# The layer norm, gating sums and beta projection between a feed-forward and a linear attention moved into the attention's first units, and the next layer norm moved into its last steps

## The chip, the cores and the metric

The kernel runs on one core of one Trainium2 chip. The metric is the device time of one execution in microseconds (us). The kernel before took 1204.1 us in the median of three runs, from 1202.74 to 1205.73 us.

## The reference

The input is x, four batches of 512 tokens with 256 features. Four layers are added to it one after the other, and each but the third reads a layer norm of x:

```python
x = x + attn_a(layernorm(x))      # 16 heads of 16, softmax over a batch
x = x + ffn(layernorm(x))         # feed-forward "b"
x = x + attn_b(layernorm(x))      # linear attention, 16 heads of 128
x = x + ffn(layernorm(x))         # feed-forward "d"
```

The feed-forward routes each token to two of eight experts, but its result is added to only eight rows of x (rows 0 to 7 of batch 0, since the scatter is by expert number): `out.at[indices[:, k]].add(gates[:, k] * silu(silu(x w1) w3) w2)`. So the kernel sums the gated hidden rows by expert first, and multiplies by w2 only eight rows.

The linear attention projects q, k, a gate and v, passes q and k through a causal convolution with four taps, a silu and a layer norm over the head, and keeps a state `S = (1 - b) S + b v k` with `b = sigmoid(x Wb + bb)` for each head and token; the output is `S q`, times the silu of the gate, times Wo.

## The kernel before, in words

Tokens stand on 128 partitions: x_tok holds 16 tiles of 128 tokens, four tiles to a batch. The normed x is kept transposed, as xn_hi and xn_lo (two parts of an fp32 number, and a product of two such numbers takes three matmuls). Each stage is a block in which five engines run their own list of instructions in the order in which the code writes them, with semaphores between them. At a block's end all engines meet at a barrier. PE is the matmul engine, ACT the scalar engine, DVE the vector engine, POOL is GpSimd, and SP issues DMAs.

A layer norm (`layer_norm`, L61) goes in groups of one batch: `statistics` on DVE (four BN_STATS, L83, and four BN_AGGR, L86), `deviations` on POOL (a power of -0.5, L96 and L98), `normalise` on DVE (L106), `transpose` on PE (L130), `high_parts` on ACT (L116) and `low_parts` on DVE (L121).

The stages that matter here, in order:

- `norm_and_ffn` with tag b (L868). PE ends with the products of w3 (L992), then the gated sums (L1020, 32 matmuls), their transpose (L1026), and the product with w2 (L1030); DVE adds the eight rows to x_tok (L1124).
- All semaphores are cleared, with a barrier (L1812).
- `norm_and_decay` (L1127). Tile 0 of x_tok is normed again, since its rows changed. For the batches 1, 2, 3, 0, PE projects beta (L1184), ACT takes the sigmoid (L1198), PE turns it to token order (L1172), DVE forms 1 - b and its running products (L1211, L1217), and SP writes them to keep_rows in DRAM (L1157).
- `linear_attention` (L1260). 64 units: 8 pairs of heads, and in a pair 8 units (batch and head of the pair). The work of a unit is spread over 7 steps, so that step u does the projections of unit u (L1477, L1490), transposes u-1 (L1504) and u-2 (L1511), scores u-2, reads out u-3 (L1555, L1558), multiplies by Wo for u-5 (L1579) and adds u-6 to x_tok (L1707). "Step" and "unit" are counted from 0, so the steps 64 to 69 are the drain, in which no projection is left.
- `norm_and_ffn` with tag d. It starts with the statistics of batches 0 and 1 on DVE; PE's first products are the router's (L960) for batch 0, then come the transposes of batch 1 and the products of w1 (L980). The transposes of batches 2 and 3 lie between later products.

In the linear attention one chain goes from unit to unit: ACT normalises q and k of unit u-1 (L1612), PE turns them back (L1511), ACT applies the affine part (L1628) and scales the projection by the first tap (L1595), DVE adds the other taps (L1679), PE transposes, DVE takes the statistics (L1718), and POOL forms the scales (L1399 to L1413), for which ACT waits to normalise the next. Two waits of DVE's gating step matter for the drain (`gated` is a single buffer):

```python
if has(u, 3):
    v, r = u - 3, (k - 3) % 4
    wait(dve, read_out, v + 1)
    wait(dve, gate_act, v + 1)
    wait(dve, gated_lo_done, v)
    dve.tensor_tensor(gated[:], outp[:], gate[:, r, :], ALU.mult).then_inc(gated_done, 1)
```

`gated_high` on ACT (L1635) and `gated_low` on POOL (L1451) split that buffer for the product with Wo.

## Time and profile before

| | us |
|---|---|
| median of three runs | 1204.1 |
| the profiled execution, its own time | 1201.73 |
| span in its profile | 1199.9 |
| feed-forward b, from its first matmul | 295.67 |
| first instruction of `norm_and_decay` | 341.93 |
| first matmul of the linear attention | 355.66 |
| last addition of the linear attention begins | 1146.48 |
| first statistics of feed-forward d | 1147.49 |
| first router matmul of feed-forward d | 1156.24 |

The last six rows are points on the profile's time axis, counted from the span's start. The span is the time from the first to the last recorded instruction; the profiled execution took 1.83 us more than its span. PE is busy for 1131.8 of 1199.9 us, but a share like that is a mean over stages: it is nearly full in the middle of the linear attention and has gaps where one stage hands over to the next.

### The profile page before, as it was taken

To read this page: it belongs to the slowest core of one execution; us is meant where nothing else is said; L and a number is where in the kernel's file an instruction comes from. 1 tells how busy PE (TensorE), PEld (TensorE's weight loads), DVE (VectorE), ACT (ScalarE), POOL (GpSimd) and SP (SyncE) were. 2 spreads that over 40 slices of the span, in tenths; PEclk is the share of its full clock that TensorE was granted. 3 is DMA by queue.
4 is the path that set the end of the run, shared out by engine and by line. 5 is a ranking of instruction groups with operands and counts; after the bars stand their busy time and mean duration, and the time that the engine had idled before them with its cause. 6 is when DMAs were issued, how large, how long until landed. Compare 5 with 4: busy or idle time off the path is not lost. (4 is left out here: it accounts for less than half of the span.)

```text
span 1199.9 us, 22451 instructions
## 1 busy us (share of the span) xinstructions
PE 1131.8 (94%) x7558; PEld 909.3 (76%) x7558; DVE 923.5 (77%) x2124; ACT 772.1 (64%) x1533; POOL 634.6 (53%) x1078
## 2 busy tenths in 40 slices
PE   8999999888977999999999999999999999999768
PEld 7444434337646899999999999999999999999646
DVE  6888877846437788888888888888888888888452
ACT  3377767772436776777676777676777777776323
POOL 4020500001703777786777786777787687767520
PEclk9899999998989999999999999999999999999989
DMA  6434434401111012101110201111211211111020
GB/s 181 54 54 55 54 54 55 54 2 37 77 34 56 31 47 68 47 32 51 63 47 32 82 32 47 67 48 32 81 35 45 76 38 43 35 47 33 16 70 1
DMA packets 23449, 60.50 MB, mean 50 GB/s; under 512 B 3367, under 2 KB 8359, under 8 KB 22183
## 3 DMA queue, kind: packets, MB, share of 16 engines
q1 hardware_dynamic: 23335, 59.07, 18.9%
q8 instruction: 61, 1.00, 0.4%
q14 instruction: 53, 0.43, 0.1%
HBM read 44.67 MB, written 2.33 MB: 39 GB/s over the span
## 5 line engine op out<-in xcount | busy, mean ns | idle before, releaser
L1679 DVE SCALAR_TENSOR_TENSOR ln_xn<-l_proj_q,par,ln_xn 128x511 f32<-128x511 f32 (+2 forms) x192 | 142.6, 742 | 113.1 <-ACT ln_xn L1595 110.8
L688 DVE TENSOR_REDUCE a_neg_max<-a_scores 128x1 f32<-128x512 f32 x244 | 155.1, 683 | 38.6 <-PE a_scores L416 36.8
L607 ACT ACTIVATE a_probs<-a_scores_t 128x512 f32<-128x512 f32 x256 | 138.4, 600 | 61.0 <-PE a_scores_t L435 60.0
L1601 ACT ACTIVATE ln_xn<-ln_xn,par 128x512 f32<-128x512 f32 x128 | 92.5, 723 | 91.2 <-DVE ln_xn L1679 91.2
L1421 POOL TENSOR_TENSOR l_k_tok<-l_normed,k_norm 128x384 f32<-128x384 f32 x64 | 64.9, 1014 | 157.9 <-ACT l_normed L1612 157.9
L1679 DVE SCALAR_TENSOR_TENSOR ln_xn<-l_proj_k,par,ln_xn 128x511 f32<-128x511 f32 (+2 forms) x192 | 143.0, 745 | 4.5
L1612 ACT ACTIVATE l_normed<-l_turn_q,l_shift,l_scale 128x128 f32<-128x128 f32 x256 | 96.3, 457 | 26.1 <-POOL l_shift L1413 26.0
L1411 POOL TENSOR_TENSOR l_scale<-l_small,l_minus_half 128x8 f32<-128x8 f32 x64 | 105.0, 1641 | 5.0
L1612 ACT ACTIVATE l_normed<-l_turn_k,l_shift,l_scale 128x128 f32<-128x128 f32 x256 | 97.1, 481 | 0.0
L1555 PE MATMUL l_outp<-l_masked,l_values 128*128 128x128 f32 x512 | 88.6, 275 | 0.9 <-DVE x_tok L1707 0.9
L1654 ACT ACTIVATE l_gate<-l_proj_gv 128x512 f32<-128x512 f32 x64 | 38.2, 597 | 79.0 <-PE l_proj_gv L1477 79.0
L1686 DVE TENSOR_TENSOR_SCAN l_decay<-l_keep,ident 128x128 f32<-128x128 f32 x256 | 87.2, 403 | 0.0
L1451 POOL TENSOR_TENSOR l_gated_lo<-l_gated,l_gated_hi 128x512 fp32r<-128x512 f32 x64 | 82.4, 1288 | 7.3 <-ACT l_gated_hi L1635 7.3
L435 PE MATMUL a_scores_t<-a_stack 50*128 50x512 f32 x256 | 73.4, 490 | 7.8 <-ACT a_probs L607 5.4
L1490 PE MATMUL l_proj_gv<-head_hi,xn_hi 128*128 128x256 f32 x256 | 76.6, 299 | 2.1 <-ACT l_gate L1654 2.1
L1579 PE MATMUL l_outp<-wo_hi,l_gated_hi 128*128 128x256 f32 x256 | 72.9, 285 | 4.1 <-DVE l_gated L1736 2.4
L89 POOL MEMSET ln_minus_half<- 128x4 f32 x3 | 0.3, 101 | 141.0 <-POOLq L170 135.2
L1558 PE MATMUL l_outp<-l_q_late,l_state 128*128 128x128 f32 x384 | 74.2, 275 | 0.0
L435 PEld LDWEIGHTS a_scores_t<-a_stack 50*128 50x128 f32 x256 | 28.5, 184 | 60.0 <-ACT a_probs L607 40.0
L1555 PEld LDWEIGHTS l_outp<-l_masked,l_values 128*128 128x128 f32 x512 | 72.7, 192 | 1.1 <-issue 1.1
L96 POOL TENSOR_SCALAR ln_var_eps<-ln_mean_var 128x4 f32<-128x4 f32 x12 | 3.0, 254 | 133.0 <-DVE ln_mean_var L79 94.2
L1497 PEld LDWEIGHTS l_scores<-l_qk 128*128 128x128 f32 x512 | 67.5, 193 | 6.5 <-issue 1.5
(321 smaller groups left out, 3606.9 us busy)
## 6 DMA issues: line engine op xcount, KB each, us to landing
l_keep<-keep_rows SPq DMA_DIRECT2D x64, 448.0 KB, 3.6
a_stack<-a_dense SPq DMA_DIRECT2D x90, 128.0 KB, 5.1
head_raw<-w_heads SPq DMA_DIRECT2D x8, 1024.0 KB, 6.7
x_tok<-x SPq DMA_DIRECT2D x4, 512.0 KB, 8.6
wo_raw<-w_o SPq DMA_DIRECT2D x1, 2048.0 KB, 11.4
out<-x_tok SPq DMA_DIRECT2D x1, 1920.0 KB
a_stack<-a_max_rows_t SPq DMA_DIRECT2D x64, 4.0 KB
ctx_tok<-w_qkv SPq DMA_DIRECT2D x1, 768.0 KB, 7.0
```

Of the source, the lines that this page charges most:

```text
L435: pe.matmul(scores_t[q % TURNS][:], half_rows(k_stack[i], e, STACK + 2)[:, slot, t * P:(t + 1) * P], half_rows(q_stack[i], e, STACK + 2)[: ...
L607: act.activation(probs[:, n % 2, h, :], scores_t[(4 * n + h) % TURNS][:], ACT.Exp, scale=SOFT_SCALE).then_inc(probs_done, 1)
L688: dve.tensor_reduce(neg_max[:, g % 2, at:at + 1], max_bank(g, j), AX.X, ALU.max, negate=True).then_inc(max_done, 1)
L1411: pool.tensor_tensor(scale[:, i, :], small[:, 7, :], minus_half[:], ALU.pow).then_inc(scales_ready, 1)
L1451: pool.tensor_tensor(gated_lo[:, k % 4, :], gated[:], f32(gated_hi[:, k % 4, :]), ALU.subtract).then_inc(gated_lo_done, 1)
L1490: last = pe.matmul(proj_gv[:, t * PAIR:(t + 1) * PAIR], lhs, rhs, start=(j == 0), stop=(j == 3 * KD - 1))
L1555: last = pe.matmul(outp[:, tok], values[:, c % 2, t, e * DK:(e + 1) * DK], masked[:, m, tok], start=True, stop=(t == 0))
L1558: last = pe.matmul(outp[:, tok], state[:, m, t - 1, :], q_late[:, m, (t - 1) * P:t * P], start=False, stop=True)
L1601: act.activation(conv[:, w, m, :], conv[:, w, m, :], ACT.Silu, bias=par[:, h, 2 * TAPS + w:2 * TAPS + w + 1]).then_inc(act_sem[w], 1)
L1612: last = act.activation(normed[:, w, t, :], turn[w][:, t * P:(t + 1) * P], ACT.Identity, scale=scale[:, m, j:j + 1], bias=shift[:, m, j:j ...
L1679: ins = dve.scalar_tensor_tensor(conv[:, w, m, s:], proj[w][:, 0:SEQ - s], par[:, h, tap:tap + 1], conv[:, w, m, s:], ALU.mult, ALU.add)
L1686: last = dve.tensor_tensor_scan(decay[:, tok], keep[:, r, tok], ident[:], 0.0, ALU.mult, ALU.add)
```

## The change

`norm_and_decay` is gone, and its work is written into the first steps of `linear_attention`. Feed-forward b ends after its gates: the gated sums, their transpose, the product with w2 and the addition to x_tok are written into step 0 of the linear attention. Hidden rows, slots and the fold matrix live on through the barrier (`carried`), and the two parts of beta's weights are made inside feed-forward b (one ACT and one DVE instruction). In the pairs 0 to 6 the batches come in the order 1, 2, 3, 0, so that batch 0, which waits for the sums, is needed last; in the last pair they come in the order 0, 1, 2, 3.

By step: step 0 has beta of batch 1 (projection, sigmoid, turn, running products), the gated sums, fold and expert rows, and the statistics of tile 0. Step 1 has the rest of tile 0's norm, the beta projections of batches 2, 3 and 0, and at ACT's end of the step their three sigmoids. Step 2 has the twelve turns of beta on PE, and DVE forms the running products of one batch in each of the steps 2, 3 and 4, each followed by SP's write to DRAM and, in SP's queue, by the load that reads it back.

At the other end, the layer norm of feed-forward d (`ln_d`) is set up before the linear attention, and batches 0, 1 and 2 are normed in the steps 64 to 69 and right behind them. Feed-forward d then starts at its router and norms only batch 3.

```diff
 def linear_attention(...)
+        def batch_of(u):
+            place = u % BODY // 2
+            return place if u >= UNITS - BODY else beta_order[place]
...
         @block.gpsimd
+                if u == 1:
+                    ln.deviations(pool, 0)
+                if u == UNITS + 1:
+                    ln_d.deviations(pool, 0)
...
             steps(step, 4)
+            for g in range(1, NB - 1):
+                ln_d.deviations(pool, g)
...
         @block.tensor
+            def project_beta(b):
+                tok, j = slice(b * SEQ, (b + 1) * SEQ), 0
+                for kd in range(KD):
+                    for lhs, rhs in split_passes(beta_hi[:, kd, :], beta_lo[:, kd, :], xn_hi[:, kd, tok], xn_lo[:, kd, tok]):
+                        last = pe.matmul(beta_bank[b][0:LH, :], lhs, rhs, start=(j == 0), stop=(j == 3 * KD - 1))
+                        j += 1
+                last.then_inc(beta_z, 1)
...
             def step(pair, k, u, of):
+                if u in (UNITS + 2, UNITS + 4):
+                    ln_d.transpose(pe, (u - UNITS - 2) // 2, proj)
+                if u == 0:
+                    project_beta(1)
...
+                    if u == 0 and w == 0:
+                        turn_beta(1, chunks)
+                if u == 0:
+                    sum_gated()
...
+                if u == 1:
+                    ln.transpose(pe, 0)
...
+                if u == 0:
+                    fold_sums()
+                if u == 1:
+                    wait(pe, rows_added, 1)
+                    project_beta(2)
+                    wait(pe, ln.lo_done, KD)
+                    project_beta(3)
+                if u == 2:
+                    for b in beta_order[1:]:
+                        turn_beta(b, outp)
...
+                if u == 0:
+                    expert_rows()
+                if u == 1:
+                    project_beta(0)
...
             steps(step, 6)
+            ln_d.transpose(pe, NB - 2, proj)
...
         @block.scalar
+                if u == 0:
+                    sigmoid(1)
+                if u == UNITS + 2:
+                    ln_d.high_parts(act, 0, proj)
...
+                if u == 1:
+                    for b in beta_order[1:]:
+                        sigmoid(b)
...
         @block.vector
+                if u == 1:
+                    ln.normalise(dve, 0)
+                if u == UNITS + 5:
+                    ln_d.normalise(dve, NB - 2)
+                if u in (2, 3, 4):
+                    keep_of(beta_order[u - 1])
...
+                if u in (UNITS + 2, UNITS + 4):
+                    ln_d.low_parts(dve, (u - UNITS - 2) // 2, proj)
+                if u in (UNITS + 1, UNITS + 3):
+                    ln_d.normalise(dve, (u - UNITS - 1) // 2)
+                if u in (UNITS, UNITS + 2, UNITS + 4):
+                    wait(dve, added, UNITS - BODY + 2 * ((u - UNITS) // 2 + 1))
+                    ln_d.statistics(dve, (u - UNITS) // 2)
```

ACT's list before, from the end of step 1 into step 2 of the linear attention (L1612 normalises unit 0, L1628 and L1595 are the affine part and the first tap that follow):

```order
L1654 ACTIVATE l_gate<-l_proj_gv 128x512
L1601 ACTIVATE ln_xn<-ln_xn,par 128x512 x2
L1612 ACTIVATE l_normed<-l_turn_q,l_shift,l_scale 128x128 x4
L1612 ACTIVATE l_normed<-l_turn_k,l_shift,l_scale 128x128 x4
L1628 ACTIVATE l_qk<-l_turn_q,norm 128x512
L1595 ACTIVATE ln_xn<-l_proj_q,par 128x512
L1628 ACTIVATE l_qk<-l_turn_k,norm 128x512
L1595 ACTIVATE ln_xn<-l_proj_k,par 128x512
```

ACT's list now, at the same place (the line numbers have shifted, L1630, L1646 and L1613 are the same three; L1657 is the sigmoid):

```order
L1684 ACTIVATE l_gate<-l_proj_gv 128x512
L1619 ACTIVATE ln_xn<-ln_xn,par 128x512 x2
L1630 ACTIVATE l_normed<-l_turn_q,l_shift,l_scale 128x128 x4
L1630 ACTIVATE l_normed<-l_turn_k,l_shift,l_scale 128x128 x4
L1657 ACT_TABLE_LOAD
L1657 ACTIVATE hidden<-l_outp,beta_bias 16x512
L1657 ACTIVATE hidden<-l_chunks,beta_bias 16x512
L1657 ACTIVATE hidden<-l_scores,beta_bias 16x512
L1646 ACTIVATE l_qk<-l_turn_q,norm 128x512
L1613 ACTIVATE ln_xn<-l_proj_q,par 128x512
L1646 ACTIVATE l_qk<-l_turn_k,norm 128x512
L1613 ACTIVATE ln_xn<-l_proj_k,par 128x512
```

Two high parts of tile 0 have come in ahead of the gate, and a table load and three sigmoids stand between the normalising and the affine part; a second table load brings the silu back.

DVE's list before, from step 65 of the drain into feed-forward d (L1736 gates, L1697 carries the state, L1707 adds to x_tok, L1278 and L1064 are the block's end and the next one's beginning):

```order
L1736 TENSOR_TENSOR l_gated<-l_outp,l_gate 128x512
L1697 SCALAR_TENSOR_TENSOR l_state<-l_state,l_keep,l_chunks 128x128 x2
L1707 TENSOR_TENSOR x_tok<-l_outp,x_tok 128x512
L1736 TENSOR_TENSOR l_gated<-l_outp,l_gate 128x512
L1707 TENSOR_TENSOR x_tok<-l_outp,x_tok 128x512 x3
L1278 UNCONDITIONAL_BRANCH
L1064 UNCONDITIONAL_BRANCH
L83 BN_STATS ln_stats<-x_tok 128x6 x4
L86 BN_AGGR ln_mean_var<-ln_stats 128x2 x4
L83 BN_STATS ln_stats<-x_tok 128x6 x4
L86 BN_AGGR ln_mean_var<-ln_stats 128x2 x4
L106 TENSOR_SCALAR ln_xn<-x_tok,ln_mean_var,ln_rstd 128x256 x4
```

DVE's list now, from the end of step 65 (L106) into step 69 (L1768 adds to x_tok, L1812 gates):

```order
L106 TENSOR_SCALAR ln_xn<-x_tok,ln_mean_var,ln_rstd 128x256 x4
L1768 TENSOR_TENSOR x_tok<-l_outp,x_tok 128x512
L1812 TENSOR_TENSOR l_gated<-l_outp,l_gate 128x512
L121 TENSOR_TENSOR xn_lo<-l_proj_q,xn_hi 128x512
L121 TENSOR_TENSOR xn_lo<-l_proj_k,xn_hi 128x512
L83 BN_STATS ln_stats<-x_tok 128x6 x4
L86 BN_AGGR ln_mean_var<-ln_stats 128x2 x4
L1768 TENSOR_TENSOR x_tok<-l_outp,x_tok 128x512
L106 TENSOR_SCALAR ln_xn<-x_tok,ln_mean_var,ln_rstd 128x256 x4
L1768 TENSOR_TENSOR x_tok<-l_outp,x_tok 128x512
L121 TENSOR_TENSOR xn_lo<-l_proj_q,xn_hi 128x512
L121 TENSOR_TENSOR xn_lo<-l_proj_k,xn_hi 128x512
```

What stood behind the four last additions now stands between them: normalise, low parts and statistics of one batch after the other.

## Rows read from the trace of the kernel before

**Rows 1.** Busy time in stretches; columns: stretch, length, busy and count per engine, clock, DMA.

```profile
335.00:356.00 21.00, 13.51 (x85) 6.03 (x84) 9.27 (x29) 6.06 (x11) 1.19 (x6) 0.87 0.06 11
...
411.00:1111.00 700.00, 698.72 (x5056) 645.58 (x5055) 597.20 (x1414) 505.50 (x1029) 522.61 (x911) 1.00 0.15 49
...
355.60:360.50 4.90, 4.84 (x12) 3.82 (x13) 0.99 (x2) 0.69 (x1) 0.15 (x2) 0.50 0.79 188
...
1156.20:1158.80 2.60, 2.56 (x7) 0.87 (x8) 2.60 (x12) 0.00 (x0) 0.85 (x2) 0.50 0.02 6
```

**Rows 2.** Timeline from feed-forward to linear attention; columns: start, duration, engine, line, operation.

```profile
335.38 1.08 ACT L1062 ACTIVATE f_hidden_b<-f_mid_b 128x512 f32<-128x512 f32 x2
...
335.68 1.93 PE L1020 MATMUL f_sums_b<-f_hidden_b,f_slots_b 128*32 128x256 f32 x32 [0.32 <-DVE f_slots_b L1118]
...
339.10 1.03 PE L1030 MATMUL f_sums_b<-w,f_summed_t_b 128*8 128x256 f32 x4 [0.27 <-DVE f_summed_t_b L1122]
...
340.17 0.41 DVE L1124 TENSOR_TENSOR x_tok<-f_sums_b,x_tok 8x256 f32<-8x256 f32 x1 [1.12 <-PE f_sums_b L1030]
...
341.93 0.20 POOL L1162 MEMSET d_zeros<- 16x128 f32 x1 [14.79 <-POOLq L1812]
...
349.36 0.68 ACT L1198 ACTIVATE d_beta_rows<-d_z,beta_bias 16x512 f32<-16x512 f32 x1 [1.16 <-PE d_z L1184]
...
352.36 1.04 DVE L1217 TENSOR_TENSOR_SCAN d_keep<-d_keep,d_zeros 16x128 f32<-16x128 f32 x3
...
355.66 0.77 PE L1477 MATMUL l_proj_q<-xn_hi,head_hi 128*128 128x512 f32 x1 [3.32 <-PEq L1131]
```

**Rows 3.** Stretch with the six matmuls of one beta projection, line 1184 alone.

```profile
347.76:349.12 1.36, 1.36 (x6) 0.48 (x6) 1.00 0.25 42
```

**Rows 4.** Timeline of the first four units of the linear attention.

```profile
361.77 1.28 ACT L1654 ACT_TABLE_LOAD   x1
...
363.06 0.60 ACT L1654 ACTIVATE l_gate<-l_proj_gv 128x512 f32<-128x512 f32 x1
...
365.20 0.39 PE L1477 MATMUL l_proj_q<-xn_hi,head_hi 128*128 128x512 f32 x1
...
376.07 0.66 PE L1511 MATMUL l_turn_q<-ident,l_normed 128*128 128x128 f32 x4 [3.32 <-ACT l_normed L1612]
...
378.95 1.54 DVE L1679 SCALAR_TENSOR_TENSOR ln_xn<-l_proj_q,par,ln_xn 128x511 f32<-128x511 f32 x2 [3.53 <-ACT ln_xn L1595]
...
387.52 0.75 PE L1511 MATMUL l_turn_q<-ident,l_normed 128*128 128x128 f32 x4 [2.37 <-ACT l_normed L1612]
```

**Rows 5.** Timeline of the last steps of the linear attention.

```profile
1135.29 1.28 POOL L1451 TENSOR_TENSOR l_gated_lo<-l_gated,l_gated_hi 128x512 fp32r<-128x512 f32 x1 [3.47 <-ACT l_gated_hi L1635]
...
1139.00 0.69 DVE L1736 TENSOR_TENSOR l_gated<-l_outp,l_gate 128x512 f32<-128x512 f32 x1 [1.98 <-PE l_outp L1558]
...
1146.48 0.69 DVE L1707 TENSOR_TENSOR x_tok<-l_outp,x_tok 128x512 f32<-128x512 f32 x1 [1.83 <-PE l_outp L1579]
```

**Rows 6.** Timeline of the start of the second feed-forward.

```profile
1147.49 1.41 DVE L83 BATCH_NORM_STATS2 ln_stats<-x_tok 128x6 f32<-128x256 f32 x4 [0.32 <-PEq L1278]
...
1149.66 1.04 POOL L98 TENSOR_TENSOR ln_rstd<-ln_var_eps,ln_minus_half 128x4 f32<-128x4 f32 x1
...
1150.73 1.40 DVE L106 TENSOR_SCALAR ln_xn<-x_tok,ln_mean_var,ln_rstd 128x256 f32<-128x256 f32 x4
...
1153.01 1.08 ACT L116 ACTIVATE xn_hi<-f_xt_d 128x512 fp32r<-128x512 f32 x2 [12.65 <-PE f_xt_d L130]
...
1154.91 1.28 DVE L121 TENSOR_TENSOR xn_lo<-f_xt_d,xn_hi 128x512 fp32r<-128x512 f32 x2
...
1156.24 0.59 PE L960 MATMUL f_sums_d<-xn_hi,w_in_hi 128*8 128x512 f32 x1 [3.05 <-DVE xn_lo L121]
...
1158.77 1.33 PE L130 MATMUL f_xt_d<-ident,ln_xn 128*128 128x128 f32 x8
...
1164.52 1.09 PE L130 MATMUL f_xt_d<-ident,ln_xn 128*128 128x128 f32 x8
```

More of the change, by code:

```diff
@@ L885, in norm_and_ffn @@
         hidden_t = sb("hidden_t", [P, KD, NB * SEQ])
-        hidden = sb("hidden", [P, NT, D])
+        if carried:
+            hidden, slots, fold, beta_w, beta_hi, beta_lo = carried
+        else:
+            hidden = sb("hidden", [P, NT, D])
+            slots = sb("slots", [P, NT, SLOT])
+            fold = sb("fold", [P, NE])
         logit_rows = sb("logit_rows", [NE, 2, SEQ])
@@ L1034, in _ @@
         def _(act):
-            if done == 0:
-                ln.high_parts(act, 0, xt)
+            if carried:
+                act.activation(beta_hi[:], beta_w, ACT.Copy).then_inc(beta_hi_done, 1)
             def copy_logits(g):
@@ L1043, in _ @@
             copy_logits(0)
-            ln.high_parts(act, 1, xt)
+            if done < 2:
+                ln.high_parts(act, 1, xt)
             for g in range(NB + 1):
@@ L1065, in _ @@
         def _(dve):
-            for g in range(counted, 2):
+            for g in range(counted, begin):
                 ln.statistics(dve, g)
```

261 lines of the change are left out of this document (145 added, 116 removed).

## The prediction

> **What bounds the kernel now.** I read the busy time by stretches first. From 411 to 1111 us, most of the linear attention, PE is busy for 698.72 of 700 us at the full clock (1.00) [rows 1]. The change alters no instruction of a unit there, only the order of the batches, so I cost the middle at nothing; what can move are its two ends. From 335 to 356 us PE is busy for 13.5 of 21 us, much of that in pieces that wait for each other [rows 1].
>
> Then I read the timeline of the first end. The last hidden rows of feed-forward b are done at 335.38 + 1.08 = 336.46 us, PE's first projection of the linear attention starts at 355.66, and the gated sums, the expert rows, a barrier, the beta stage and a second barrier lie between [rows 2]. Of the units behind them the reader is to see what PE waits for: the turn back of unit 0 starts at 376.07 after 3.32 us of idle and that of unit 1 at 387.52 after 2.37, both released by ACT's normalising [rows 4]. So the first units are bound by the chain ACT, DVE, POOL, ACT of one unit after the other, with a period of 387.52 - 376.07 = 11.45 us, and not by PE's work.
>
> Last, the second end: the last addition ends at 1146.48 + 0.69 = 1147.17, the statistics start at 1147.49, and the first router matmul at 1156.24, released by a low part on DVE [rows 5, 6]. From 1156.2 to 1158.8 the granted clock is 0.50, that is 1.2 GHz [rows 1].
>
> **The start of the linear attention.** The barrier between them comes 341.93 - (340.17 + 0.41) = 1.35 us after the last work [rows 2]. The same cost behind 336.46 puts the new start at 337.8 us, against 355.66: 17.85 us earlier. What that must pay for comes back in the steps:
>
> Step 0, up to the first projection of unit 1, took 365.20 - 355.66 = 9.54 us [rows 2, 4]. PE now has in its list: six beta matmuls, six for q, four turns, six for k, 32 for the gated sums, six for the gate, two products for the fold, twelve for the values, and the expert rows. Before, the first 4.9 us ran at half clock with twelve matmuls done [rows 1], that is about 0.41 each, and six beta matmuls at full clock take 1.36 us [rows 3]. PE will again come out of a pause, so I let the half clock fall on beta and q now: 2.5 + 2.4, then 0.3 for the turns, 1.4 for k, 1.93 for the sums [rows 2], 1.4 for the gate's projection, 0.9 of wait for ACT's gate (0.60 [rows 4] and its release), in which the fold hides, 1.5 for the values, and 0.9 of the 1.03 for the expert rows [rows 2]: 13.2 us. Step 0 is 3.7 us longer. ACT loads the sigmoid table behind beta's matmuls and the silu table behind k's, so neither is on this path. DVE's running products of batch 1 (1.04 [rows 2] and one operation ahead of them) end before the first tap of q arrives.
>
> Step 1, from there to the turn back of unit 0, took 376.07 - 365.20 = 10.87 us. It gains the norm of tile 0: DVE waits for POOL's power at its start, where it would have waited for the first tap anyway, and two short low parts stand in front of the taps of k. For a whole batch, from statistics to normalising, that wait is 1150.73 - 1147.49 = 3.24 us, the upper end; nothing is the lower. Eighteen beta matmuls on PE (3 x 1.36 = 4.1 us [rows 3]) fit mostly into PE's 3.32 us of idle [rows 4] and its wait for ACT's gate. I take 1.0 us longer, as only a tile is normed and part is hidden.
>
> From there to the turn back of unit 1, the 11.45 us are the chain itself. ACT now has a table load of 1.28 and three sigmoids of 0.68 us between normalising unit 0 and the affine part and first tap of unit 2 [rows 2, 4]: 1.28 + 3 x 0.68 = 3.3 us, all of it in the chain, since DVE already waits 3.53 us for that tap [rows 4]. PE's twelve turns of beta (about 1.2 us) lie in the idle that this makes. Step 2 is 3.3 us longer.
>
> The running products in the steps 2 to 4 cost DVE about 1.45 us each (1.04 and the operation ahead), and stand where it waits 3.53 us for the tap: nothing, as long as that wait is there; without it, 1.45 us each. In the steps 2 to 4 each load of SP stands behind a write in its queue, but still about a unit ahead of the scan that reads it, so I cost SP at nothing; late by a whole period it would be 11.45 us.
>
> Sum of this end: 17.85 - (3.7 + 1.0 + 3.3) = 9.85 us gained. The ends of it: PE's inserted work is 5.4 (beta) + 1.4 (turns) + 1.9 + 0.5 + 0.9 + 0.3 = 10.4 us; were none of it hidden and ACT's 3.3 on top, 17.85 - 13.7 = 4.1 is left. Were ACT's 3.3 hidden and one half clock stretch less, 17.85 - 4.7 + 2.4 = 15.5.
>
> The Trainium skill ("ScalarE: Activation LUTs", What ACT_TABLE_LOAD costs) gives a drain of about 1.38 us on top of the 1.28 for each switch of table. Here the gate starts at 363.06, right at the end of the load that began at 361.77 [rows 4], so I add no drain. By the page the sigmoids would put 4.7 instead of 3.3 us into the chain, and the whole would be 1193.8 instead of 1192.4 us.
>
> **The drain and the start of feed-forward d.** The statistics of batch 0 (step 64) and its normalising (step 65) stand on DVE where it waits for scores, and delay the fourth last addition by 0.2 us. Then ACT's high parts of batch 0 (1.08 [rows 6]) stand ahead of the split of unit 62's gated rows, and wait for the transposes, which end at about 1137.1. So POOL's low part of unit 62, now 1135.29 to 1136.57 [rows 5], comes at 1138.9 to 1140.15, and DVE's gating of unit 63 waits for it: 1140.2 instead of 1139.00 [rows 5]. From its end at 1140.9 DVE is one chain:
>
> - low parts of batch 0, 1.28: 1142.2
> - statistics of batch 1 to its normalising, with POOL's power between: 1150.73 - 1147.49 = 3.24 [rows 6], in which an addition (0.69) hides: 1145.4
> - normalise, 1.40: 1146.8; the next addition, 0.69: 1147.5; the low parts wait for transposes and high parts (1.08) and end at about 1148.9
> - statistics of batch 2 to its normalising, 3.24: 1152.2; normalise: 1153.6; last addition: 1154.3; low parts behind the high parts: 1155.8
> - the block's end, 1147.49 - 1147.17 = 0.32: 1156.1, and the router starts at 1156.2.
>
> That is where it starts now (1156.24). What stays gained is inside feed-forward d: the transposes of batch 1 between the router and the first product of w1 (at 1158.77, 1.33 us long, of which the next product waits about 1.1) and those of batch 2 (at 1164.52, 1.09 long, about 0.85 of wait) [rows 6]. Against them stands a half clock that may last somewhat longer, as in the 4.9 us at the attention's start: 2.6 us of it lie on the router already [rows 1], and 0 to 1 us more is to be paid. DVE norms batch 3 by about 1161, and PE wants it only behind the third router product. Sum of this end: 1.9 gained, from -1.5 (each of the three rounds 1.1 late) to +3.
>
> **Sum.** 9.85 + 1.9 = 11.7 us. The profiled execution took 1201.73 us (span 1199.9 and 1.83 around it), so 1190.0 by its own time. It is 2.4 us below the median of the runs shown, 1204.1, and I forecast the median: 1192.4 us.
>
> **The rivals.**
>
> *PE pays for everything.* If the chain of the first units has no room for PE's 10.4 us, the start yields 4.1 and the whole 6.0 us: 1198.1. For it speaks that PE is full from 411 us on; against it the 3.32 and 2.37 us of idle in front of the turns back.
>
> *The sigmoids hide, or the clock stays up.* Then the start yields up to 15.5 us: 1186.7. For it: the beta matmuls are dense work that PE does before the projections. Against it: DVE's wait for the tap, which names ACT.
>
> *The drain costs more than it saves.* If DVE's chain in the drain is a further 3.4 us longer, the end yields -1.5 instead of 1.9: 1195.8. For it: three rounds, each with two handovers and POOL's power in line.
>
> *Slower: the middle stretches.* The new order of batches, tiles at new addresses and SP's loads could lengthen each unit. There are 60 units behind step 3, and 11.7 / 60 = 0.2 us each takes all; from 0.25 us a unit it is slower by over 0.3%, for instance 0.3 us each gives 1210. Against it: a unit's time there is PE's own work, with 698.72 of 700 us busy, and PE's instructions in a unit are the same and in the same order.
>
> *It doesn't do what it says:* the start is held by something else at the barrier (SP's DMAs, POOL's split of Wo). POOL was idle for 14.79 us before 341.93, so done by 327.1 [rows 2], and the beta stage's own memory write is gone; only a much longer clearing of semaphores would do it, and leave the time within 0.3%.
>
> **How the numbers follow.** Forecast 0.58 (1189 to 1195.5 by itself), PE pays 0.12, sigmoids or clock 0.15, costlier drain 0.08, stretched middle 0.03, nothing changed 0.04. A change of 0.3%, 3.6 us, is about what a measurement of this kernel can tell from none. Faster by more than that: 0.92, since PE's rival keeps 6.0 us and the drain's 8.3, less a remainder; within it 0.05; slower 0.03. The range for 8 in 10 reaches to both neighbours, 1187 to 1198.
>
> **What would show it.** In the changed profile the linear attention's first matmul is at 337.8 us (later means the barrier), unit 1's first projection at 351.0, the turns back of units 0 and 1 at about 363 and 377.5. PE's wait for the transposes of unit 1 names ACT's affine part, behind the sigmoids. DVE's waits in the drain name POOL's power, the router starts within 1 us of 1156.2 - 9.85 = 1146.4 on the new axis, and the first product of w1 comes right behind it. The forecast is wrong if the turn back of unit 1 is before 374 or behind 381, if the router starts over 3 us from there, or if the 700 us of the middle are no longer full.

## The result, and the profile after

The changed kernel takes 1192.73 us (median of six runs, 1187.74 to 1193.23), the kernel before 1203.57 in the same session: a ratio of 0.9905, 95% interval 0.9882 to 0.9927. The forecast was 1192.4. The profiled execution has a span of 1190.9 us, 9.0 less than the 1199.9 of before, and took 1192.82.

The first stretch of the linear attention, from the timeline of the changed kernel (start, duration, engine, line, operation, idle before and who ended it):

```profile
336.18 1.08 ACT L1070 ACTIVATE hidden<-f_mid_b 128x512 f32<-128x512 f32 x2
...
338.65 0.39 PE L1473 MATMUL l_scores<-xn_hi,beta_hi 128*16 128x512 f32 x1 [2.49 <-PEq L1905]
...
350.23 0.50 PE L1432 MATMUL l_proj_q<-xn_hi,head_hi 128*128 128x512 f32 x1
...
361.54 0.66 PE L1466 MATMUL l_turn_q<-ident,l_normed 128*128 128x128 f32 x4
...
376.62 0.66 PE L1466 MATMUL l_turn_q<-ident,l_normed 128*128 128x128 f32 x4 [1.00 <-ACT l_normed L1630]
...
389.09 0.66 PE L1466 MATMUL l_turn_q<-ident,l_normed 128*128 128x128 f32 x4 [1.85 <-ACT l_normed L1630]
```

These answer to [rows 2, 4]. PE starts 1.39 us behind ACT's last hidden rows (337.26) and issues six beta products, each 0.23 us behind the one ahead. That is full speed, where I had put a half clock. Unit 1's first projection follows 11.6 us later, the turn back of unit 0 at 361.54, that of unit 1 at 376.62.

The stretches of the same kernel (length, busy time and count on PE, PEld, DVE, ACT, POOL, granted clock, DMA share, GB/s):

```profile
338.60:350.20 11.60, 11.21 (x80) 7.34 (x80) 7.08 (x14) 6.52 (x8) 0.27 (x4) 1.00 0.42 117
...
415.00:1111.00 696.00, 694.03 (x5027) 641.97 (x5026) 592.69 (x1405) 500.11 (x1019) 518.41 (x902) 1.00 0.15 49
...
1148.10:1151.00 2.90, 2.89 (x7) 1.28 (x8) 1.69 (x8) 0.14 (x1) 1.03 (x2) 0.50 0.70 233
```

PE is still full in the middle. The router still starts at 0.50, that is 1.2 GHz, as in [rows 1].

ACT around the turns of units 0 and 1, DVE there and a step later, and POOL beside it:

```profile
361.37 1.51 ACT L1630 ACTIVATE l_normed<-l_turn_k,l_shift,l_scale 128x128 f32<-128x128 f32 x4
362.90 1.28 ACT L1657 ACT_TABLE_LOAD   x1
364.19 0.68 ACT L1657 ACTIVATE hidden<-l_outp,beta_bias 16x512 f32<-16x512 f32 x1
...
365.92 0.75 ACT L1646 ACTIVATE l_qk<-l_turn_q,norm 128x512 f32<-128x512 f32 x1
366.58 0.66 ACT L1613 ACTIVATE ln_xn<-l_proj_q,par 128x512 f32<-128x512 f32 x1
...
368.49 1.28 ACT L1684 ACT_TABLE_LOAD   x1
```

```profile
365.35 1.04 DVE L1743 TENSOR_TENSOR_SCAN hidden<-hidden,ident 16x128 f32<-16x128 f32 x3
...
376.27 1.36 DVE L1721 TENSOR_TENSOR_SCAN l_decay<-l_keep,ident 128x128 f32<-128x128 f32 x4
377.55 0.39 DVE L1740 TENSOR_SCALAR hidden<-hidden 16x512 f32<-16x512 f32 x1
377.97 2.59 DVE L1743 TENSOR_TENSOR_SCAN hidden<-hidden,ident 16x128 f32<-16x128 f32 x3
380.49 1.50 DVE L1714 SCALAR_TENSOR_TENSOR ln_xn<-l_proj_q,par,ln_xn 128x511 f32<-128x511 f32 x2
```

```profile
378.04 1.15 POOL L1370 TENSOR_TENSOR l_k_tok<-l_normed,k_norm 128x384 f32<-128x384 f32 x1 [3.81 <-ACT l_normed L1630]
379.15 1.14 POOL L1375 TENSOR_TENSOR l_q_late<-l_qk,l_keep 128x384 f32<-128x384 f32 x1
```

The same place on ACT in the kernel before, and its wait on DVE one step later, ahead of the taps of unit 3:

```profile
375.89 1.51 ACT L1612 ACTIVATE l_normed<-l_turn_k,l_shift,l_scale 128x128 f32<-128x128 f32 x4
377.26 0.82 ACT L1628 ACTIVATE l_qk<-l_turn_q,norm 128x512 f32<-128x512 f32 x1
```

```profile
391.68 1.53 DVE L1679 SCALAR_TENSOR_TENSOR ln_xn<-l_proj_q,par,ln_xn 128x511 f32<-128x511 f32 x2 [3.59 <-ACT ln_xn L1595]
```

The table load and the sigmoids stand between normalising and the affine part, as forecast: from the start of the one to the start of the other it was 377.26 - 375.89 = 1.37 us and is 365.92 - 361.37 = 4.55. The surprise is on DVE: the same three scans that take 1.04 us at 365.35 take 2.59 at 377.97, while POOL works on tiles in SBUF. No wait is left ahead of the taps at 380.49, where the kernel before had one of 3.59 us.

The drain, DVE first, then ACT and POOL, and the router on PE:

```profile
1132.33 0.69 DVE L1812 TENSOR_TENSOR l_gated<-l_outp,l_gate 128x512 f32<-128x512 f32 x1 [3.09 <-POOL l_gated_lo L1400]
...
1137.28 1.38 DVE L106 TENSOR_SCALAR ln_xn<-x_tok,ln_mean_var,ln_rstd 128x256 f32<-128x256 f32 x4 [0.90 <-POOL ln_rstd L98]
...
1144.07 1.38 DVE L106 TENSOR_SCALAR ln_xn<-x_tok,ln_mean_var,ln_rstd 128x256 f32<-128x256 f32 x4 [1.47 <-POOL ln_rstd L98]
```

```profile
1129.75 0.59 ACT L116 ACTIVATE xn_hi<-l_proj_k 128x512 fp32r<-128x512 f32 x1
1130.23 0.63 ACT L1653 ACTIVATE l_gated_hi<-l_gated 128x512 fp32r<-128x512 f32 x1
```

```profile
1130.93 1.26 POOL L1400 TENSOR_TENSOR l_gated_lo<-l_gated,l_gated_hi 128x512 fp32r<-128x512 f32 x1 [8.35 <-ACT l_gated_hi L1653]
```

```profile
1148.11 0.59 PE L965 MATMUL f_sums_d<-xn_hi,w_in_hi 128*8 128x512 f32 x1 [2.17 <-PEq L1195]
```

These answer to [rows 5, 6]. Unit 63's gating waits for POOL's low part of unit 62, which waits for ACT's copy, which stands behind the high parts of batch 0: the chain of the forecast. The router is at 1148.11, 8.13 earlier than in [rows 6].

One profile isn't enough for a microsecond here. So I cut every profile of this study at five points: the start of ACT's last hidden rows in feed-forward b (H), the turns back of units 5 and 63, the router's first and PE's last matmul. All in us, each read from a timeline:

```
kernel (by label)        H       H to u5   u5 to u63   u63 to router   router to last
before                   335.38  100.93    688.96      30.97           40.49
changed                  336.18   90.78    689.06      32.09           39.62
changed, second profile  334.21   91.04    689.53      32.01           39.58
e1, start only           333.86   90.74    689.60      32.48           41.24
e11, start only again    336.42   90.77    690.92      31.79           40.91
e2, end only             336.96  100.84    688.70      33.14           39.45
e3, split first          334.40   90.78    690.79      31.42           39.39
e4, silu betas           331.90   88.09    690.55      31.40           39.09
e5, products later       336.73   91.00    689.44      32.06           39.61
e6, norm earlier         334.64   90.67    689.53      22.72           38.19
e7, e5 and e6            336.93   92.25    689.43      22.72           38.16
e8, tanh                 330.66   86.84    688.36      31.40           39.08
e9, zeros in PSUM        334.88   89.29    689.10      31.57           39.29
e10, e6, e8 and e9       331.45   85.33    688.33      22.71           38.17
```

H moves by 6.3 us among kernels that are the same up to there but for the two parts of beta's weights, and the 58 units of the middle by 2.6. Neither belongs to the edits. The columns between are what the experiments are read from. Of the 9.0 us between the first two rows, H gives back 0.8, the start gains 10.15, the middle loses 0.1, the drain loses 1.1 and the last feed-forward gains 0.9.

### The profile page after: what moved, and what is told of

Read it like the earlier page. It is cut to its first block and busy times, and to the rows that moved or that the text cites. A ratio compares the mean times of both kernels' runs of the same rounds, so it can differ in the third digit from the quotient of the medians.

```text
span 1190.9 us, 22446 instructions
## 1 busy us (share of the span) xinstructions
PE 1132.6 (95%) x7558; PEld 910.8 (76%) x7558; DVE 929.5 (78%) x2126; ACT 773.4 (65%) x1535; POOL 635.5 (53%) x1077
## 5 line engine op out<-in xcount | busy, mean ns | idle before, releaser
L1630 ACT ACTIVATE l_normed<-l_turn_q,l_shift,l_scale 128x128 f32<-128x128 f32 x256 | 96.3, 457 | 25.8 <-POOL l_shift L1362 25.8
L1630 ACT ACTIVATE l_normed<-l_turn_k,l_shift,l_scale 128x128 f32<-128x128 f32 x256 | 97.1, 480 | 0.0
L96 POOL TENSOR_SCALAR ln_var_eps<-ln_mean_var 128x4 f32<-128x4 f32 (+1 forms) x13 | 3.0, 231 | 152.8 <-DVE ln_mean_var L79 94.4
```

What stands on the lines that cost most here:

```text
L1630: last = act.activation(normed[:, w, t, :], turn[w][:, t * P:(t + 1) * P], ACT.Identity, scale=scale[:, m, j:j + 1], bias=shift[:, m, j:j ...
```

## The experiments

Theory at the outset: the start carries the gain, and the end gives nothing. Rivals: the end is worth its forecast 1.9 us, or it costs.

**Start alone, twice.** Every step of `linear_attention` that uses `ln_d` is taken out, and feed-forward d norms all batches again:

```diff
-        norm_and_ffn(nc, semaphore, "d", ..., ln_d, (NB - 1, NB - 1), out=out)
+        norm_and_ffn(nc, semaphore, "d", ..., ln_d, (0, 0), out=out)
```

> The changed kernel's start (no separate norm-and-decay stage) with the old end: nothing of the second feed-forward's layer norm runs in the linear attention's drain. My theory, that the whole gain comes from the start and the end gives nothing: 9 to 10 us under the kernel before, so a profile span of 1190 to 1191.5 us, level with the changed kernel's 1190.9 or 0.3 below it; the first turn of unit 63 near 1116.0 as there, the first router product of the last feed-forward within 0.5 us of 9.3 before the old kernel's 1156.24. Rival, that the end is worth its forecast 1.9 us: 1192.5 to 1193 us of span. Rival, that the end costs over a microsecond: 1189.5 us or less.

> The changed kernel's start with the old end once more, for the size of the end's term, which one profile of each can't give since half-clock stretches fall differently. If the new end is worth the forecast 1.9 us, the time is 2 us over the changed kernel's 1192.5 and the distance from unit 63's turn to the last product 73 to 74 us as in the first profile of this kernel (73.7, against 71.6 to 71.7 in three profiles of the changed end). If it is worth nothing, 1192 to 1193 us and a distance of 71.5 to 72 us.

Measured: 0.9930 of before (0.9903 to 0.9956) and 0.9921 (0.9893 to 0.9949), medians 1194.39 and 1195.36 beside 1205.15 and 1205.48. H to unit 5 is that of the changed kernel, 90.74 and 90.77 us. From unit 63 to the last matmul it takes 73.72 and 72.70 us; the distance of e11 lies between what its two theories expected. The spans can't decide: e1's 1191.1 us fits "the end gives nothing", but its H is 2.3 us earlier than in the changed kernel's first profile, and in e11's session the kernel before was slower too.

**End alone.** The drain's lines put into the kernel before, with (3, 3) for its feed-forward d.

> The old start (separate norm-and-decay stage), with batches 0 to 2 of the last layer norm in the linear attention's drain. My theory: within 1 us of the kernel before (span 1199.0 to 1200.5 us); the last feed-forward's first router product stands 0.5 to 1.2 us later than the old 1156.24, counted from the same unit 63, and the transposes no longer needed after it give that back. Rival, the forecast's own term: 1.9 us faster, the router at 1156.2. Rival, dearer drain: 2 us slower.

Measured: 0.9987 (0.9971 to 1.0004), 1203.91 us beside 1205.15: a gain of 1.2 us, which the interval doesn't tell from none. H to unit 5 is 100.84, as before. The way to the router is 33.14 us, 2.2 longer than in the profile of before, and from there to the end it is 1.0 shorter.

**The changed kernel again.**

> The changed kernel once more, unaltered, to see how far one profile of it stands from another and to time it beside the next three. The kernels run so far spend 8 to 13 us of the 71 us behind unit 63's first turn at half clock, in one to three stretches that don't stand in the same places from profile to profile. If that is chance and not code, this profile differs from the first one (32.1 us from unit 63's turn to the first router product, 71.7 to the last product) by up to 2 us at equal instructions, and the time is 0.988 to 0.993 of the kernel before. If the places are fixed by the code, both distances repeat within 0.3 us.

Measured: 0.991 (0.9885 to 0.9934), 1192.34 us. From unit 63 on both distances repeat within 0.1 us (32.01, 39.58), which by my own sign would mean places fixed by the code; but e4, e8 and e9, whose drain is the same code, take 31.40 to 31.57 us to the router. And the steps at the start don't repeat. Step 2 takes 16.56 us here and 15.08 in the first profile, step 5 11.91 against 13.49. Step 2 is the way from the turn back of unit 0 to that of unit 1, and so on. The two profiles over step 5, the first one first:

```profile
401.60:415.10 13.50, 13.47 (x86) 12.25 (x87) 10.03 (x25) 9.46 (x20) 9.57 (x16) 0.87 0.11 34
```

```profile
401.20:413.10 11.90, 11.90 (x87) 11.01 (x87) 9.67 (x25) 8.87 (x19) 9.57 (x16) 1.00 0.12 39
```

The same instructions take 1.6 us more at a mean clock of 0.87 than at 1.00. Over steps 2 to 5 the sum is 53.58 us in one profile (u0 361.54, u4 415.12) and 53.49 in the other (359.60, 413.09). Step 2 has a stretch of half clock in both; in the second it lasts longer, at a mean clock of 0.79 against 0.89 over the step, and step 5 has none. It needn't be one or the other: e7 takes 16.56 us in step 2 and 13.18 in step 5, and its H to unit 5 is the longest of the changed starts, 92.25.

In the drain the time moves too. From unit 63's turn to the router, for the kernel before, e1, e11 and e2:

```profile
1125.30:1156.20 30.90, 16.78 (x106) 14.53 (x106) 14.15 (x44) 5.80 (x12) 11.71 (x14) 0.83 0.21 68
```

```profile
1114.20:1146.70 32.50, 18.41 (x107) 16.07 (x108) 14.22 (x44) 5.82 (x12) 11.75 (x14) 0.81 0.20 65
```

```profile
1118.10:1149.90 31.80, 18.01 (x107) 15.59 (x107) 14.20 (x44) 5.85 (x12) 11.74 (x14) 0.79 0.20 66
```

```profile
1126.50:1159.60 33.10, 20.52 (x122) 18.44 (x122) 17.05 (x46) 7.88 (x16) 10.54 (x12) 0.76 0.00 0
```

The first three have the same code there and differ by 1.5 us. So the old end is 71.46, 73.72 or 72.70 us long (mean 72.6), and the changed end, in the seven profiles that have it unaltered, 70.48 to 72.59 (mean 71.3): 1.3 us gained, with ranges that overlap. Cut at the router it is clearer. From there to the last matmul the old end takes 40.49 to 41.24 us and the changed one 39.08 to 39.62 (means 40.9 and 39.4): 1.5 us gained, and no profile of the one reaches the other. The way to the router is 30.97 to 32.48 with the old end and 31.40 to 33.14 with the changed one (means 31.75 and 31.95), which can't be told apart.

The times decide nothing. By the ratios (the means of two each) the end is worth (0.9926 - 0.9908) x 1204 = 2.2 us, with intervals that overlap; by the medians the start alone gains 10.76 and 10.12 us and the changed kernel 10.84 and 9.96, which leaves nothing for the end. So the change does gain behind the router, and what the whole end gives stays open between nothing and 2.2 us; the forecast's 1.9 is within that, and no closer figure is shown.

**Which copy holds unit 63's gating.**

```diff
-                if u == UNITS + 2:
-                    ln_d.high_parts(act, 0, proj)
                 if has(u, 2):
                     norm_affine(u - 2, (k - 2) % BODY, 0)
...
                 if has(u, 4):
                     gated_high(u - 4, (k - 4) % BODY)
+                if u == UNITS + 2:
+                    ln_d.high_parts(act, 0, proj)
```

> The changed kernel with one order altered on ScalarE: in the second step after the last unit the rounding copy of unit 62's gated rows goes ahead of the two copies of layer-norm batch 0. If those two copies are what held GpSimd's low part and so VectorE's gating of unit 63 (its wait of 3.09 us), gating starts about 2.5 us earlier (from 1132.3 to near 1129.8) and everything to the router moves up by some 1 to 2.5 us, the span from 1190.9 to 1189 to 1190. If the copies merely filled time in which ScalarE had to wait for something else, gating moves by under 0.5 us and the batch 0 split, now later, makes the router the same or up to 0.5 us later.

One execution. DVE from the gating of unit 62 to that of unit 63, then POOL:

```profile
1125.43 0.69 DVE L1812 TENSOR_TENSOR l_gated<-l_outp,l_gate 128x512 f32<-128x512 f32 x1 [3.28 <-PE l_outp L1571]
...
1126.67 2.37 DVE L106 TENSOR_SCALAR ln_xn<-x_tok,ln_mean_var,ln_rstd 128x256 f32<-128x256 f32 x4
1128.96 0.68 DVE L1768 TENSOR_TENSOR x_tok<-l_outp,x_tok 128x512 f32<-128x512 f32 x1
1131.62 0.69 DVE L1812 TENSOR_TENSOR l_gated<-l_outp,l_gate 128x512 f32<-128x512 f32 x1 [1.98 <-PE l_outp L1571]
```

```profile
1126.86 1.39 POOL L1400 TENSOR_TENSOR l_gated_lo<-l_gated,l_gated_hi 128x512 fp32r<-128x512 f32 x1 [4.32 <-ACT l_gated_hi L1653]
```

The changed kernel, the gating of unit 62 and PE's last products ahead of the gating of unit 63:

```profile
1126.01 0.69 DVE L1812 TENSOR_TENSOR l_gated<-l_outp,l_gate 128x512 f32<-128x512 f32 x1 [3.82 <-PE l_outp L1571]
```

```profile
1130.79 0.39 PE L1571 MATMUL l_outp<-l_q_late,l_state 128*128 128x128 f32 x2
```

In e3 POOL's low part comes 4.0 us earlier, counted from unit 63's turn, and DVE no longer waits for it but for PE's products. Yet from the gating of unit 62 to that of unit 63 it takes 1131.62 - 1125.43 = 6.19 us, against 1132.33 - 1126.01 = 6.32 in the changed kernel and 5.14 in the kernel before and in e1: 0.13 us gained where I had expected 2.5. In the changed kernel PE's products are done at 1131.18, so the low part holds the gating by 1.1 us. Without that hold e3 should have gained about as much. But its low part runs beside the normalising, which takes 2.37 us instead of 1.38; PE's transposes wait for that, and its products end 6.2 us behind the gating of unit 62 instead of 5.2. What was gained at one place was lost at the other. The router is at 31.42 us behind unit 63, 0.7 sooner than in the first profile; most of that comes ahead of unit 62's gating, which the edit doesn't reach, and e4 and e8 have 31.40 without the edit.

**No table exchange.** First with a scaled SiLU in place of the sigmoid for batches 2, 3 and 0, which leaves out the bias and gives other decays than the reference, then with the sigmoid's own value written as tanh (the diff):

```diff
-                act.activation(beta_rows[b], ..., ACT.Sigmoid, bias=beta_bias[:]).then_inc(beta_done, 1)
+                act.activation(beta_rows[b], ..., ACT.Tanh, scale=0.5, bias=half_bias[:]).then_inc(beta_done, 1)
...
-                dve.tensor_scalar(kept[b][:, 0:SEQ], beta_rows[b], -1.0, 1.0, ALU.mult, ALU.add).then_inc(kept_first, 1)
+                dve.tensor_scalar(kept[b][:, 0:SEQ], beta_rows[b], -0.5, 0.5, ALU.mult, ALU.add).then_inc(kept_first, 1)
```

> The changed kernel with the learning rates of batches 2, 3 and 0 put through a scaled SiLU without bias instead of the sigmoid (the output changes by it), so that the function table isn't exchanged at unit 1 and back at unit 2. My theory: the table loads of 1.28 us at 362.90 and at 368.49 go; the first stands in the chain from the normalised k rows to the tap of unit 2, so step 2 (turn of unit 0 to turn of unit 1) goes from 15.08 to about 13.8 us, the span from 1190.9 to about 1189.6. If the skill's 1.38 us of drain besides were paid too, step 2 would be near 12.4. Rival, that ScalarE's load is hidden behind the beta products: step 2 stays at 15.0.

> The changed kernel with each learning rate computed as half of one plus tanh of half the argument, the same value as the sigmoid: the factors go into the existing operations, and one small operation halves the bias. Tanh lies in the table set that SiLU uses, so none of the linear attention's four table loads is left. My theory, from the SiLU kernel: step 2 (turn of unit 0 to turn of unit 1) takes 12.4 to 12.7 us instead of 15.0 to 16.5, and from the last copy of the first feed-forward to unit 3's turn it is 2 to 3 us shorter than the 65.45 us of the first profile of the changed kernel; time 2 to 3 us under its 1192.5. Rival, that part of the SiLU kernel's 2.5 us came from chance in the clock: step 2 takes 13.5 or more.

Measured: SiLU, one execution, step 2 of 12.56 us; tanh, 0.9858 (0.9818 to 0.9898), 1188.40 us beside 1205.48, step 2 of 12.82. The interval overlaps that of the changed kernel, so the time alone doesn't show a gain; the step does. ACT in the tanh kernel:

```profile
355.82 1.51 ACT L1633 ACTIVATE l_normed<-l_turn_k,l_shift,l_scale 128x128 f32<-128x128 f32 x4
357.19 0.66 ACT L1660 ACTIVATE hidden<-l_outp,l_half_bias 16x512 f32<-16x512 f32 x1
```

From the normalised k rows to the first of the three operations it is 1.37 us here and 364.19 - 361.37 = 2.82 in the changed kernel: the exchange costs ACT 1.45 us. The other 0.8 of step 2 went with the half clock: the granted clock over the step is 1.00 here and 0.89 there. The second load, at 368.49, isn't in the way: behind it ACT waits 1.89 us more for PE's product. The 12.56 us of e4 lie where I had put them for a drain on top of the load (12.4), and that number alone would have misled; e4's own rows have the same 1.37 us on ACT (357.04 to 358.41), and its clock is at 1.00 too. Part of the 3.9 us on H to unit 5 (86.84) is that no dip fell into step 5 of e8 either, and that part I can't call shown. The span of 1179.5 owes 5.5 us to an early H.

The Trainium skill ("ScalarE: Activation LUTs", What ACT_TABLE_LOAD costs) has about 2.66 us for a switch, load and drain. The rows give 1.45, so the measurement decides against the drain, as in the prediction. The same page (Table sets: the hidden batching unit) advises to batch calls by set; here the load vanished by choosing a function of the set that was already there.

**The slow scans.** Moved behind the state updates; and in their old place, with the zeros that they add read from PSUM:

```diff
-                if u in (2, 3, 4):
-                    keep_of(beta_order[u - 1])
+                if u == 2:
+                    keep_of(beta_order[1])
...
+                if u in (3, 4):
+                    keep_of(beta_order[u - 1])
                 if has(u, 0):
                     b, half = k // 2, k % 2
```

```diff
+        psum_zeros = chunks[0:LH, SEQ - P + LH:SEQ - P + LH + 1].to_broadcast([LH, P])
...
-                                                  zeros, 1.0, ALU.mult, ALU.add)
+                                                  zeros if i < 2 else psum_zeros, 1.0, ALU.mult, ALU.add)
```

> The changed kernel with VectorE's running products of batches 3 and 0 (three scans each, 2.59 us at 377.97 and 390.50 beside GpSimd's two-input work, 1.04 us for the same three scans at 341.48) moved from the head of units 3 and 4 to behind the state updates, ahead of the values product. My theory, that the scans share a port with GpSimd's late rows and delay the taps: the scans take 1.0 to 1.3 us each time and steps 2 and 3 (turn to turn of units 1 to 3) go from 12.47 and 12.54 to 11.6 to 11.9, together 1.2 to 1.7 us off the span. Rival, that VectorE has as much to do in its new place or GpSimd is busy there too: steps stay at 12.2 or more and the span moves by under 0.5 us.

> The changed kernel with the zeros that the running products of batches 3 and 0 add read from PSUM instead of SBUF, so that these scans have one SBUF input, in the same place of VectorE's order. My theory, that two SBUF inputs on VectorE and GpSimd's two-input work block each other: the three scans take 1.0 to 1.3 us instead of 2.59, and steps 2 to 3 and 3 to 4 go from 12.47 and 12.54 to 11.5 to 11.8 us each, some 1.5 us off the time. Rival, that any scan beside GpSimd's work is slow, or that the delay is elsewhere: scans stay over 2.3 us and the steps at 12.4.

For e9 PE also writes the zeros in step 1, and its state products in the steps 3 and 4 wait for the scans. In e9 and e10 batch 3's beta product overwrites the place of the zeros before the scans read it, so the decays of batches 3 and 0 differ from the reference. A version with a place that nothing overwrites would have the same scans; none was run.

Moved, DVE and POOL of e5:

```profile
380.01 1.53 DVE L1714 SCALAR_TENSOR_TENSOR ln_xn<-l_proj_q,par,ln_xn 128x511 f32<-128x511 f32 x2 [1.88 <-ACT ln_xn L1613]
...
388.61 1.04 DVE L1743 TENSOR_TENSOR_SCAN hidden<-hidden,ident 16x128 f32<-16x128 f32 x3
...
390.17 3.69 DVE L1721 TENSOR_TENSOR_SCAN l_decay<-l_keep,ident 128x128 f32<-128x128 f32 x4
```

```profile
390.08 1.01 POOL L1370 TENSOR_TENSOR l_k_tok<-l_normed,k_norm 128x384 f32<-128x384 f32 x1 [1.78 <-ACT l_normed L1630]
391.05 1.14 POOL L1375 TENSOR_TENSOR l_q_late<-l_qk,l_keep 128x384 f32<-128x384 f32 x1
```

The products are back at 1.04 us, and now the decay scan behind them meets POOL: 3.69 us instead of 1.36. Step 3, between the turns of units 1 and 2, fell from 12.47 to 11.53 us, and step 4 rose from 12.54 to 13.73. Time 0.9906 (0.9889 to 0.9922), nothing gained. In PSUM, DVE and POOL of e9:

```profile
378.10 1.03 DVE L1751 TENSOR_TENSOR_SCAN hidden<-hidden,l_chunks 16x128 f32<-16x128 f32 x3
379.57 1.53 DVE L1720 SCALAR_TENSOR_TENSOR ln_xn<-l_proj_q,par,ln_xn 128x511 f32<-128x511 f32 x2 [0.44 <-ACT ln_xn L1619]
```

```profile
378.10 1.02 POOL L1372 TENSOR_TENSOR l_k_tok<-l_normed,k_norm 128x384 f32<-128x384 f32 x1 [5.22 <-ACT l_normed L1636]
```

Same scans, same moment, same work on POOL, one SBUF input less: 1.03 us. Steps 3 and 4 are 11.55 and 11.89 instead of 12.47 and 12.54, together 1.57 us shorter, and POOL's own product takes 1.02 instead of 1.15. That it is the second SBUF input of these scans which collides is thereby shown. The two rows of taps tell what the forecast missed: with nothing ahead of it the wait for the tap of unit 3 is 1.88 us (e5), products of 0.42 + 1.04 us fit into it and leave 0.44 (e9), and at 0.42 + 2.59 they don't. Time 0.9886 (0.9850 to 0.9922), which by itself doesn't tell 1.6 us.

The Trainium skill ("SBUF — State Buffer", Who interferes with whom) calls the pair of ports that VectorE and GpSimd share an exclusive lock, and says that a VectorE instruction with two SBUF inputs contends with a GpSimd instruction that reads SBUF, as does one in a two-port mode. The traces of the scans agree (2.59 against 1.03 us). The normalising of e3 has one SBUF input and went from 1.38 to 2.37 us; whether it runs in a two-port mode, no run here shows. I had not held the scans' two inputs against this rule when I costed them.

**The norm one step sooner.**

```diff
+                if u == UNITS + 1:
+                    ln_d.normalise(dve, 0)
+                    wait(dve, added, UNITS - 4)
+                    ln_d.statistics(dve, 1)
+                    ln_d.low_parts(dve, 0, proj)
                 if has(u, 2):
                     ...
                     dve.tensor_tensor(masked[:, k % 2, :], scores[:], decay[:], ALU.mult).then_inc(masked_done, 1)
+                if u == UNITS + 1:
+                    ln_d.normalise(dve, 1)
...
-        norm_and_ffn(nc, semaphore, "d", ..., ln_d, (NB - 1, NB - 1), out=out)
+        norm_and_ffn(nc, semaphore, "d", ..., ln_d, (3, 2), out=out)
```

> The changed kernel with the drain's layer norm one step sooner: batch 0 wholly and batch 1's normalising in the step behind the last unit, batch 1's transposes one step on, and batch 2 only up to its deviations, its normalising and transposes left to the last feed-forward beside its own products. My theory, that from unit 63's gating on the drain is a chain on VectorE and GpSimd in which the layer norm's steps stand in line with the attention's own: the first router product of the last feed-forward comes 6 to 8 us sooner (25 to 26 us behind unit 63's turn, not 32.1) and the span falls by 5 to 8 us to 1183 to 1186; of that up to 2 us are lost again where batch 2's and 3's norms are late for the feed-forward. Rival, that the attention's own last products and the last add set the router: it moves by under 2 us and the span by under 1.

> Both edits together, the running products behind the state updates and the layer norm one step sooner. The two places are 700 us apart and share nothing, so the gains add: span 1182 to 1185 us and 0.980 to 0.985 of the kernel before if both theories hold; by the two rivals 1190 us.

Batch 0 is normed wholly in step 65 and batch 1 only as far as its normalising; batch 1's transposes follow in step 66, and batch 2 has only its statistics and deviations in the drain. Feed-forward d norms the rest of it beside its own products. PE's, ACT's and POOL's lists are changed to match.

Measured: 0.9837 (0.9804 to 0.9869), 1183.43 us beside 1202.3; with e5's edit as well 0.9826 (0.9801 to 0.9851), 1181.92, which isn't told from e6. The router of e6 and the stretch ahead of it:

```profile
1137.56 0.40 PE L965 MATMUL f_sums_d<-xn_hi,w_in_hi 128*8 128x512 f32 x1 [1.05 <-PEq L1195]
```

```profile
1114.80:1137.50 22.70, 15.34 (x114) 13.33 (x114) 16.71 (x40) 6.95 (x14) 10.75 (x12) 1.00 0.00 0
```

It comes 22.72 us behind unit 63, 9.4 sooner than in the changed kernel and more than the 6 to 8 that I had expected, and the way from it to the end is 1.4 shorter rather than longer: the loss that I had allowed for is not there. The clock is at 1.00 throughout. With the rounds of batches 1 and 2 no longer between the last additions, PE's longest pause is 1.78 us instead of 3.55, and the router runs at full speed, here as in e7 and e10. How much of the 9.4 us is DVE's order and how much the clock is not separated; e10's profile, at a mean of 0.92 in this stretch, has the same 22.71, so the chain and not the clock sets the router there.

**All three.**

> The layer norm one step sooner in the drain, tanh for the sigmoid, and the zeros of two batches' running products in PSUM, together. They lie in three places and each shortens its own chain: 9 us (measured, norm sooner), 2.5 and 1.5 us expected, so 1179 to 1182 us by the clock of these runs, 0.979 to 0.983 of the kernel before. If the start's two gains only shift waits to PE, which is busy without a gap from unit 6 on: 1183 to 1184 us as with the norm alone.

Measured: 0.9772 (0.9738 to 0.9805), 1179.04 us beside 1205.48. H to unit 5 is 85.33 us, that of e8 less 1.51: tanh and PSUM zeros add up. From unit 63 to the end it is e6's 60.9. The shortest version run that leaves nothing of the reference out is e7, 20.4 us under the kernel before and 10.4 under the changed one, by medians of one session. Tanh with the earlier norm, which would leave nothing out either, wasn't run without the zeros in PSUM.

## Why the prediction was right

The time was within 0.4 us, and that close is luck. The gain was forecast at 11.7 us and is 10.8 by the medians and 9.0 by the two profiles; the median of before came out 0.5 us lower than the one I subtracted from; and of the terms below some are wrong in opposite directions. What the forecast had right is the mechanism of the start.

*Start, 17.85 us earlier.* Right: 17.81, counted from H. The barrier costs 1.35 us again (337.26 to ACT's first record at 338.61).

*Step 0, 13.2 us.* 11.58 measured. Too long by 1.6: I let the half clock of [rows 1] fall on beta and q. The granted clock was 1.00.

*Step 1, 11.87 us.* 11.31 measured; tile 0's norm and the beta products of three batches together cost 0.4, not 1.0.

*Step 2, 14.75 us.* 15.08 and 16.56 us in the two profiles. ACT's term (table load and three sigmoids) was the mechanism: 4.55 - 1.37 = 3.18 us between normalising and the affine part, where I had put 3.3, the exchange being 1.45 of it. What I left out is a half clock behind the pause that it makes for PE. The changed kernel at 367 and 369 us:

```profile
367.00:369.00 2.00, 1.40 (x9) 1.19 (x8) 1.69 (x4) 1.98 (x4) 1.83 (x3) 0.75 0.17 29
369.00:371.00 2.00, 2.00 (x6) 1.59 (x6) 2.00 (x10) 0.78 (x1) 1.23 (x4) 0.50 0.00 0
```

*Running products in steps 3 and 4, nothing.* This is the term that was mis-sized. I wrote that they hide in DVE's wait "as long as that wait is there", took the 1.04 us of [rows 2], where POOL was idle, and didn't ask what POOL does at the new place. They take 2.59 us and the wait, which without them would be 1.88 (e5), is gone; that costs 1.57 us over both steps, by e9.

*Sum of the start, 9.85.* 10.15 by H to unit 5: 17.81 earlier, less 2.04 in step 0, 0.44 in step 1, 3.63 in step 2 and 1.55 in the steps 3 to 6, for which I had put 3.7, 1.0, 3.3 and nothing. Too much for step 0 and too little for the steps 3 to 6 cancel. In those last steps both kernels have one stretch of half clock (step 3 of before takes 13.13 us, step 5 of the changed one 13.49).

*Drain, router where it was.* As far as can be told: 1.1 us later by the first two profiles counted from unit 63, 0.2 by the means of all, with the profiles of either end 1.5 us or more apart. The wait for the low part, which I had put at 1.2 us, is there: from the gating of unit 62 to that of unit 63 it takes 1.18 us more than before (6.32 against 5.14). The chain on DVE was as drawn, each round with its wait for POOL's power (0.90, 1.47).

*Inside feed-forward d, 1.9 gained.* 1.5 by the means, and clear of the scatter. With the drain together the end is worth 1.3 us by profiles and between nothing and 2.2 by times.

The rivals: PE paid little of its 10.4 us. Steps 0 and 1 together took 376.07 - 355.66 = 20.41 us before and 361.54 - 338.65 = 22.89 now. The middle didn't stretch: 688.33 to 690.92 us with the new order of batches (mean of twelve 689.6), 688.70 and 688.96 with the old. The means differ by 0.01 us a unit, where that rival needed 0.2.

## What to carry to other kernels

Before work is moved to where an engine waits, read what the other engines do in that place: here scans with two SBUF inputs beside GpSimd's work took two and a half times their row from elsewhere, and one input in PSUM took that away. The same holds when you take a wait away: in e3 the freed operation ran beside another, and lengthened it by nearly what the wait had cost. A drain is a chain, so what is put in it has to be ready one step earlier than it is needed; the same layer norm brought about 2 us at most where the change put it and about 9 more one step sooner. And with a clock that dips at other places from one execution to the next, cut several profiles at the same instructions before you believe a difference of a microsecond.

## What the runs showed of the hardware

- Where TensorE is granted half clock (1.2 of 2.4 GHz) is not fixed by the program: the same instructions took 13.49 us at 0.87 in one profile and 11.91 at 1.00 in another, while step 2 had means of 0.89 and 0.79.
- After 2.49 us of idle at the barrier TensorE came back at full clock (338.65), though behind pauses of 3.32 and 3.05 us it started at half clock in the kernel before ([rows 1], 355.66 and 1156.24).
- Three scans of 16x128 take 1.04 us alone, 2.59 beside GpSimd, 1.03 beside GpSimd with one input in PSUM; four of 128x128 take 1.36 and 3.69 (e5).
- Tanh and SiLU need no table exchange between them: e8 has none of the linear attention's four loads. Sigmoid and SiLU do, at 1.45 us on ScalarE in the one place where it was measured.
